# Attention and pair convolution on one core: the outputs of 28 of 32 query chunks turned by a transposing DMA, and VectorE's work put on other steps

## The reference

```python
# layer 0: self-attention over the 4096 positions
f = einsum('kc,bcn->bkn', Wq, xf) + bq        # 32 rows
g = einsum('kc,bcn->bkn', Wk, xf) + bk        # 32 rows
h = einsum('oc,bcn->bon', Wv, xf) + bv        # 256 rows
beta = softmax(einsum('bki,bkj->bij', f, g), axis=1)
x = x + gamma * einsum('bci,bij->bcj', h, beta)
# layer 1: 32 mid channels, all 528 products of two of them, 256 outputs
y = bn_relu(w1 @ gn(x) + b1)
x = x + bn_relu(w2 @ (y[rows] * y[cols]) + b2)
```

## Time and profile before

| | before |
|---|---|
| median of 3 runs | 2097.68 us (2096.98 to 2099.1) |
| the profiled execution, its own time | 2099.17 us |
| its span, first to last instruction | 2097.4 us |
| TensorE busy | 2052.2 us, 98% |
| DVE, ACT, POOL busy | 75%, 78%, 70% |

### The profile page before, as it was taken

One profiled execution on the slowest core, in us unless ns is written; L12 is line 12 of the kernel. 1 busy time (PEld: TensorE's weight loads), 2 busy tenths in 40 slices (PEclk: granted clock), 3 DMA queues, 4 the chain that ended last, 5 costly groups with the idle time before them and its releaser, 6 DMA issues.

```text
span 2097.4 us, 48084 instructions
## 1 busy us (share of the span) xinstructions
PE 2052.2 (98%) x17334; PEld 1612.2 (77%) x17334; DVE 1571.7 (75%) x3491; ACT 1626.0 (78%) x2582; POOL 1464.8 (70%) x2110
## 2 busy tenths in 40 slices
PE   4899999999999999999999999999999999999999
PEld 3688888888877777777877777777787777877854
DVE  8787877778776776877768777776877767676667
ACT  5677877778787878888778788877787777878767
POOL 3265666657677777877768687777867767677766
PEclk9999999999999999999999999999999999999999
DMA  5165777776477797778468687787837776675632
GB/s 191 37 102 96 138 143 144 139 127 118 83 133 126 146 166 150 148 149 162 90 138 144 120 162 141 155 170 138 158 78 135 146 126 138 124 137 92 140 73 80
DMA packets 728269, 271.89 MB, mean 130 GB/s; under 512 B 674240, under 2 KB 681152, under 8 KB 728000
## 3 DMA queue, kind: packets, MB, share of 16 engines
q1 hardware_dynamic: 728032, 268.82, 66.2%
HBM read 77.07 MB, written 19.92 MB: 46 GB/s over the span
## 4 chain that ended last, share of the span: by engine, by line
PE 92%; DVE 3%; ACT 2%; issue 1%; POOL 1%; DMA 1%; SPq 0%; DVEq 0%; ACTq 0%
PE acc L1784 21%; PE acc L1772 20%; PE acc L1773 20%; PE tps L1577 5%; PE acc L1577 5%; PE sps L1597 4%; PE tps L1648 4%; PE acc L1571 3%; PE tps L1650 2%; PE acc L1648 1%; PE tps L1612 1%; PE tps L1558 1%; PE tps L1634 1%; PE acc L1650 1%; PE sps L1547 1%
## 5 line engine op out<-in xcount | busy, mean ns | idle before, releaser
L1162 POOL TENSOR_TENSOR kb<-ks,kb 128x512 f16<-128x512 f32 x630 | 750.6, 1196 | 346.6 <-ACT ks L1345 181.8
L1772 PE MATMUL acc<-hth,kt 128*128 128x257 f16 x2520 | 587.2, 273 | 0.0
L1773 PE MATMUL acc<-htl,kt 128*128 128x256 f16 x2520 | 586.6, 273 | 0.0
L1345 ACT ACTIVATE ks<-ks,kbias,esc 128x512 f32<-128x512 f32 x630 | 506.6, 805 | 0.0
L1333 ACT ACTIVATE ph<-sps,esc 128x512 f16<-128x512 f32 x394 | 269.6, 684 | 276.2 <-PE sps L1597 263.1
L863 DVE TENSOR_SCALAR_CACHE_REDUCE ks<-acc 128x512 f32<-128x512 f32 x378 | 259.6, 687 | 180.7 <-PE acc L1577 178.2
L1784 PE MATMUL acc<-hth,kt 128*128 128x257 f16 x2520 | 385.8, 274 | 0.0
L1772 PE MATMUL acc<-hth,ph 128*128 128x257 f16 x1576 | 367.4, 274 | 0.5 <-ACT ph L1333 0.5
L1773 PE MATMUL acc<-htl,ph 128*128 128x256 f16 x1576 | 366.9, 273 | 0.0
L1784 PEld LDWEIGHTS acc<-hth,kt 128*128 128x128 f16 x2520 | 247.8, 98 | 100.6
L1343 ACT ACTIVATE kb<-ks,kbias,esc 128x512 f16<-128x512 f32 x378 | 305.5, 808 | 21.9 <-DMA kt<-kb 18.3
(11 more groups left out here) (254 smaller groups left out, 3360.4 us busy)
## 6 DMA issues: line engine op xcount, KB each, us to landing
rt<-turned SPq DMA_DIRECT2D x96, 256.0 KB, 4.9
xt<-x SPq DMA_DIRECT2D x46, 512.0 KB, 4.4
xb<-x SPq DMA_DIRECT2D x32, 512.0 KB, 4.9
out<-zt SPq DMA_DIRECT2D x45, 256.0 KB, 2.7
kt<-kb SPq DMA_TRANSPOSE x630, 3.2
yb<-turned SPq DMA_DIRECT2D x36, 128.0 KB, 2.6
rt<-turned SPq DMA_DIRECT2D x72, 64.0 KB, 2.2
turned<-yb SPq DMA_DIRECT2D x12, 256.0 KB, 2.4
```

What stands on the lines that cost most here:

```text
L1162: tt(kb[:, m % KB_RING, 1], ks[:, m % KS_RING], kb[:, m % KB_RING, 0], ALU.subtract).then_inc(kl_ok, 1)
L1345: A(ks[:, m % KS_RING], ks[:, m % KS_RING], ACT.Exp, bias=kbias[:, tile % 2:tile % 2 + 1], scale=esc[:]).then_inc(kp_ok, 1)
L1772: mm(bank[:, 0:C + 1], high[:, q], hth[:, c * QT + q], start=(s8 == 0 and q == 0), stop=False)
L1773: mm(bank[:, 0:C], high[:, q], htl[:, c * QT + q], start=False, stop=False)
```

## The change

In every chunk but the last of an image (28 of 32) the output is no longer turned by TensorE. `divide` writes the fp16 high half of the scaled result into `oth` (the memory of `ot`), a new DVE instruction `output_low` writes the low half in step 5 of the next tile, and SP turns each tile by a transposing DMA into the new buffer `od` (`turn_output`, steps 21, 23 and 31, and step 7 of the next chunk). DVE then adds the high and the low half of each half of the channels to x with four instructions (`finish_turned`, steps 14, 16, 17 and 19) and takes the statistics in steps 21 and 22 (`own_stats`). `od` takes the room of one chunk of x: XR is 13 and no longer 14. The layer-1 low products move from steps 3, 4, 7, 10, 12 to 3, 5, 8, 9, 11, the statistics of the other images to steps 0, 8, 24 and some more, and the early values of the next image to steps 11, 15, 19, 26 of the last chunk with another order of chunks.

```diff
-XR = 14
+XR = 13
+        od = sb("od", [P, QT, 2 * H2, P], f16)
+        oth = ot[:].rearrange("p t c -> p (t c)").bitcast(f16).rearrange("p (t e c) -> p t e c", t=QT, e=2)
-        VORD = (4, 0, 5, 1, 6, 2, 3, 7)
+        VORD = (4, 0, 5, 3, 6, 1, 2, 7)
-        NEXT_STATS = tuple((J, t) for J, ts in ((0, (8, 11, 15)), (1, (11, 15, 21)), (2, (11, 18))) for t in ts)
-        LATER_STATS = ((2, 27), (3, 2), (3, 9), (3, 18), (3, 25), (4, 2), (4, 9), (4, 18), (4, 25), (5, 2), (5, 9), (5, 18),
-                       (6, 22), (6, 29), (7, 4), (7, 11))
+        NEXT_STATS = tuple((J, t) for J, ts in ((0, (8, 16, 24)), (1, (0, 8, 24)), (2, (0, 8))) for t in ts)
+        LATER_STATS = ((2, 24), (3, 0), (3, 8), (3, 24), (4, 0), (4, 8), (4, 24), (5, 0),
+                       (5, 8), (5, 24), (6, 0), (6, 8), (6, 24), (6, 30), (7, 4), (7, 9))
-        V_EARLY = (12, 15, 18, 21)
+        V_EARLY = (11, 15, 19, 26)
 # SP
+            def turn_output(tile):
+                G, k = divmod(tile, QT)
+                sp.wait_ge(ot_low, tiles_lowered(tile))
+                if transfers_before(G):
+                    sp.wait_ge(own_ok, 2 * H2 * transfers_before(G))
+                sp.dma_start_transpose(od[:, k], oth[:, k].rearrange("p e c -> p (e c)")).then_inc(od_in, 16)
...
+                        if J and t == 7:
+                            turn_output(QT * G - 1)
+                        if by_transfer(G) and t in (21, 23, 31):
+                            turn_output(QT * G + (21, 23, 31).index(t))
 # DVE
+            def output_low(tile):
+                k = tile % QT
+                dve.wait_ge(ot_act, tile + 1)
+                V.scalar_tensor_tensor(oth[:, k, 1], acc[tile % 2][:, 0:C], rinv[:, k:k + 1], oth[:, k, 0],
+                                       ALU.mult, ALU.subtract).then_inc(ot_low, 1)
+            def finish_turned(G, e, h):
...
+                own = xb[:, x_slot(b, J), h].rearrange("p (t q) -> p t q", t=QT)
+                V.scalar_tensor_tensor(own, od[:, :, H2 * e + h], vout[:, h:h + 1], own,
+                                       ALU.mult, ALU.add).then_inc(own_ok, 1)
...
-                        if b and n >= 1 and t in (3, 4, 7, 10, 12):
-                            product_low(n - 1, (3, 4, 7, 10, 12).index(t))
-                        if J and t in (5, 8):
-                            finish(G - 1, (t - 5) // 3, 1)
-                        if J and t in (6, 11):
-                            second_stats(G - 1, (t - 6) // 5, 1)
+                        if b and n >= 1 and t in (3, 5, 8, 9, 11):
+                            product_low(n - 1, (3, 5, 8, 9, 11).index(t))
+                        if J and t in (14, 16, 17, 19):
+                            finish_turned(G - 1, *((0, 0), (0, 1), (1, 0), (1, 1))[(14, 16, 17, 19).index(t)])
+                        if J and t in (21, 22):
+                            own_stats(G - 1, t - 21)
 # ACT, divide
+                if transfers_before(G):
+                    act.wait_ge(od_in, 16 * QT * transfers_before(G))
+                if by_transfer(G):
+                    A(oth[:, k, 0], acc[tile % 2][:, 0:C], ACT.Copy, scale=rinv[:, k:k + 1]).then_inc(ot_act, 1)
 # PE
-                            transposed(G - 1, (t - 4) // 3, 1)
...
+                            if by_transfer((tile - 2) // QT):
+                                pe.wait_ge(ot_low, tiles_lowered(tile - 2))
```

More of the change, by code:

```diff
@@ L203, in build @@
         rinv_ok = sem("rinv_ok")
-        ot_act = sem("ot_act")
+        ot_act, ot_low, od_in, own_ok = sem("ot_act"), sem("ot_low"), sem("od_in"), sem("own_ok")
         y_mm, y_ok = sem("y_mm"), sem("y_ok")
@@ L444, in product_at, with by_transfer, transfers_before, tiles_lowered @@
             return rt0[0:rows, grp] if n < SHARED else turn_bank(n, grp)[0:rows, :]
+        def by_transfer(G):
+            return G % NCH != NCH - 1
+        def transfers_before(G):
+            return G - G // NCH
+        def tiles_lowered(tile):
+            return QT * transfers_before(tile // QT) + (tile % QT + 1 if by_transfer(tile // QT) else 0)
         @block.sync
@@ L551, in _ @@
                     n = (b - 1) * NCH + J
+                    G = b * NCH + J
                     nxt = b < LASTB and 3 <= J <= 6
@@ L902, in invert, with own_stats @@
                 V.reciprocal(rinv[:, tile % QT:tile % QT + 1], acc[tile % 2][:, C:C + 1]).then_inc(rinv_ok, 1)
+            def output_low(tile):
[4 more added lines that the diff above has]
+            def finish_turned(G, e, h):
+                b, J = divmod(G, NCH)
+                if e == h == 0:
+                    dve.wait_ge(od_in, 16 * QT * (transfers_before(G) + 1))
+                    dve.wait_ge(bv_ok, G + 1)
+                if e:
+                    dve.wait_ge(own_ok, 2 * H2 * transfers_before(G) + h + 1)
+                own = xb[:, x_slot(b, J), h].rearrange("p (t q) -> p t q", t=QT)
+                V.scalar_tensor_tensor(own, od[:, :, H2 * e + h], vout[:, h:h + 1], own,
+                                       ALU.mult, ALU.add).then_inc(own_ok, 1)
+            def own_stats(G, h):
+                b, J = divmod(G, NCH)
+                dve.wait_ge(own_ok, 2 * H2 * transfers_before(G) + H2 + h + 1)
+                V.bn_stats(bst[:, h, J], xb[:, x_slot(b, J), h])
             def finish(G, h, par):
@@ L1017, in attend @@
                             invert(tile - 1)
+                        if s8 == 5 and tile and by_transfer((tile - 1) // QT) and (J or t >= NCH):
+                            output_low(tile - 1)
                         if s8 == 6 and tile + 2 < TILES:
@@ L1051, in attend @@
                             normed(("qk", b + 1, 2 * (J - 2)))
-                        if b < LASTB and J == NCH - 1 and t in (13, 16, 19, 22):
-                            normed(("v", b + 1, VORD[(13, 16, 19, 22).index(t)]))
+                        if b < LASTB and J == NCH - 1 and t - 1 in V_EARLY:
+                            normed(("v", b + 1, VORD[V_EARLY.index(t - 1)]))
             project()
@@ L1225, in _ @@
                             low(("qk", b + 1, 2 * (J - 3) + 1))
-                        if t in (14, 17, 20, 23) and b < LASTB and J == NCH - 1:
-                            low(("v", b + 1, VORD[(14, 17, 20, 23).index(t)]))
+                        if t - 2 in V_EARLY and b < LASTB and J == NCH - 1:
+                            low(("v", b + 1, VORD[V_EARLY.index(t - 2)]))
                         if t == 20 and b and 1 <= n < SHARED - 1:
@@ L1349, in divide @@
                 act.wait_ge(rinv_ok, tile + 1)
-                k = tile % QT
+                k, G = tile % QT, tile // QT
+                if transfers_before(G):
+                    act.wait_ge(od_in, 16 * QT * transfers_before(G))
+                if by_transfer(G):
+                    A(oth[:, k, 0], acc[tile % 2][:, 0:C], ACT.Copy, scale=rinv[:, k:k + 1]).then_inc(ot_act, 1)
+                    return
                 A(ot[:, k], acc[tile % 2][:, 0:C], ACT.Copy, scale=rinv[:, k:k + 1]).then_inc(ot_act, 1)
@@ L1456, in attend @@
                             high(("qk", b + 1, 2 * (J - 2)))
-                        if b < LASTB and J == NCH - 1 and t in (12, 15, 18, 21):
-                            high(("v", b + 1, VORD[(12, 15, 18, 21).index(t)]))
+                        if b < LASTB and J == NCH - 1 and t in V_EARLY:
+                            high(("v", b + 1, VORD[V_EARLY.index(t)]))
             act.wait_ge(set_dve, mark["scaled_qkv"])
```

12 lines of the change are left out of this document (6 added, 6 removed).

## The result

The changed kernel took 2118.5 us (median of 4 runs, 2116.0 to 2121.3), the kernel before 2098.4 (4 runs, 2097.0 to 2100.1) beside it: ratio 1.0096, 95% interval 1.0078 to 1.0113. It is slower by 20 us, where 12 us less were forecast.

What follows compares the result with a forecast made beforehand. TensorE, busy for 98% of the span, was taken as the bound. -24.1 + 3 + 5.4 + 1.8 + 1.8 = -12.1 us on the profiled 2097.4 gave 2085.3, stated as 2086 from the median; range 2076 to 2096.

Steps and rivals of the forecast that it cites:

- 3, 5.4, 1.8 and 1.8: Forecast losses in us: DVE's additions, early `xt` load, SP at image 0's chunk 6 to 7, chunk 1 of images 1 to 3.
- SP's new transfers: 1.24 us per issue; 1.8 us lost at image 0's chunk 6 to 7, 0.6 each at chunk 1 of images 1 to 3.
- What TensorE loses: Two groups of four transposes in each of 28 chunks, 0.43 us a group: 24.1 us, the whole gain.
- a microsecond taken from TensorE is a microsecond of the kernel: Premise for the attention: TensorE is almost never idle, so time removed there shortens the kernel in full.
- VectorE's work: Additions at 0.96 us and `output_low` at 0.45 add 116 us, taking DVE from 75% to about 81% busy.
- What it costs the end: DVE's added work, tightest in image 0's chunk 3, costs the kernel 3 us, bounds 0 and 9.
- one margin of 2.0 us: Time an unloaded DVE has between finishing a piece and TensorE writing that bank again, from 396.92 to 398.96.
- The second rival: DVE becomes the bound, additions averaging 1.6 us, deciding mean about 1.4: kernel slower, 2105 us; chance 0.08.
- The early load: Image 0, chunk 5: later `xt` load stops ACT, so TensorE waits 5.4 us (4.5 to 6.8) for `ph`.
- The third rival: SP's queue or landing holds `kt` back 0.43 us in most chunks, 12 us more: 2098, no change; chance 0.12.
- The edits costed at nothing: Waits for `output_low` and `od_in`, and the order of value chunks, taken to cost 0 us.

Runs made afterwards that it cites:

- experiment 8: experiment 3 without `output_low` and without the two low additions, so the attention's output is missing: 2082.0 us, ratio 0.9927.
- experiment 3: experiment 1 without its 112 output transfers and the waits for them, the additions reading a zeroed buffer: 2091.8 us, ratio 0.9972.
- experiment 1: The changed kernel with the last statistics of image 0's chunk 5 at step 18 instead of 24: 2112.4 us, ratio 1.0066.
- experiment 2: The kernel before plus 112 transposing transfers at the change's steps into a buffer nobody reads: 2101.7 us, ratio 1.0015.
- experiment 11: The kernel before with the x ring at 13 slots instead of 14 and the matching order of value chunks: 2117.3 us, ratio 1.0093.
- 5: experiment 1 with output transfers merged by two tiles, 56 issues instead of 112, same bytes: 2097.7 us, ratio 0.9999.
- experiment 6: experiment 1 with two additions of a turned chunk instead of four, low halves left out, all transfers kept: 2099.6 us, ratio 1.0010.
- experiment 12: experiment 1 with merged output transfers (half the issues) and the two low-half additions left out: 2087.6 us, ratio 0.9951.
- experiment 4: The kernel before with one TensorE transpose instead of four in each of 56 groups: 2085.9 us, ratio 0.9945.
- 9: The kernel of 5 with statistics moved in chunks 5 and 6, and the turned chunk's statistics in chunk 7: 2096.3 us, ratio 0.9990.
- experiment 7: The change made for only 13 chunks, the rest at the steps of the kernel before, x ring at 13: 2111.2 us, ratio 1.0062.

## Why the prediction was wrong

By runs, the change's way from 2098.4 to 2118.5 us is: 24.1 less on TensorE; 7.7 more with neither transfers nor low halves (experiment 8); 9.8 for the low halves on VectorE (3 against 8); 20.6 for the transfers (1 against 3); 6.1 for the late load (the change against 1). -24.1 + 7.7 + 9.8 + 20.6 + 6.1 = 20.1. The shares hold for this order of removal alone. Taken first, the transfers cost 3.3 us (experiment 2) and the shorter ring 19 (experiment 11); between half the issues and two additions the order matters by only 2.7 us (experiments 1, 5, 6 and 12).

The forecast was of 12 us less. The terms that it added were 3, 5.4, 1.8 and 1.8, and nothing for the rest; the runs show 9.8, 6.1, 20.6 and 7.7. The step that failed most is the price of SP's new transfers, 3.6 us against 20.6, and with it the way of adding up: each term was read against the margins of the kernel before, as if the others left them whole. For the transfers alone 3.6 was near the 3.3 of experiment 2, which lost 1.6 us in chunk 7 of image 0 (1.8 forecast) and 0.7 and 0.3 in chunk 1 of images 1 and 3 (0.6 each).

- **What TensorE loses**: right, 0.87 us a chunk. The premise with it, that "a microsecond taken from TensorE is a microsecond of the kernel", was wrong. Experiment 4 does nothing else and gives 12.4 of 18.1. An engine that is busy for 1493.93 of 1497.00 us says that no one was later than it, not by how much. Chunk 1 of images 1 to 3 did not follow; in image 1 the chain still goes through the `rt` transfer, before and in experiment 4.
- **VectorE's work**: sized well. Its groups in the changed kernel:

```profile
L947 DVE SCALAR_TENSOR_TENSOR xb<-od,vout,xb 128x512 f32<-128x512 f16 x112 | 116.3, 1038 | 0.3
L935 DVE SCALAR_TENSOR_TENSOR ot<-acc,rinv,ot 128x256 f16<-128x256 f32 x112 | 53.5, 478 | 0.0
```

  1.04 us where I took 0.96, 0.48 for 0.45. **What it costs the end** was too small: 3 us with a bound of 9, against 9.8 for the low halves alone. I counted one margin of 2.0 us, at chunk 3 of image 0, which lost nothing. The loss was in its chunks 1, 2, 5 and 7 (experiment 8), which also hold weights, moments or loaded statistics; that these take the margin is argued, not tested. The second rival did not come: its mean of 1.4 was not reached.
- **The early load**: right place, and a price of 5.4 against 6.1 in the kernel's time. That this is so near is partly luck: the stall costs 10.4 us in its own chunk, and 4.0 come back only because the next load moves too (experiment 1). I moved the load behind the spreads and forgot the two output transfers, which push the spreads too (402.02, not 397.67); I followed `ph`, while TensorE stood for `gst`, which ScalarE makes behind it; and I priced no loss of clock.
- **SP's new transfers**: the step that failed most, 3.6 us against 20.6. The price of an issue was right (1.24); I charged it at four places and not in steps 21 to 31 of chunks 3 to 6, where SyncE also issues twelve spreads and, in images 1 and 2, layer-1 transfers. The third rival's mechanism (0.12) is what came, but in a few chunks: by experiments 1 and 3, 2.0 to 4.6 us each in chunks 5 and 7 of images 1 and 2, and 3.7 in chunk 6 of image 0, not 0.43 in all.
- **The edits costed at nothing**: the ring of 13 and the order of the chunks. I looked only at the ring's effect on one load. Experiment 11 shows 19 us if nothing is moved. How the 7.7 us divide between the ring, the moves and the failed premise no run isolates. SyncE in experiment 6 is still 2.7 us later than in experiment 2 at the table's place; 2.5 of them are two plain issues that held it for 1.70 and 1.81 us, where 0.43 and 0.59 are usual. What made them long is open.

## What to carry to other kernels

When the bound engine is given less to do, its margins shrink with it: before counting the saving, read for each queue that gets new work the slack at its most crowded place (landing against use), not its mean share. Here the queue paid per issue and hardly per byte: merge transfers before moving them. And count the memory that a change takes: a ring one slot shorter can cost as much as the change was to give.

## What the chip showed beyond that

**The granted clock can halve when TensorE has stood still.** Stands of 8.59 us (changed kernel), 6.31 (experiment 11), 2.57 (9) and 2.14 (1) came with a granted clock of 0.50, the lower of the two levels, 1.2 GHz, for 10.2, 6.8, 3.4 and 3.4 us (from 405.0 and 998.5 in the two long ones, within the stand, and at its end or 1.1 us behind it in the short ones). All five stands of 5.9 us and more did so. Of the shorter ones the length alone does not decide: one of 2.03 us in experiment 7 was followed by 0.50, while this one, another of 2.27 and one of 2.27 in experiment 12 were followed by a clock of 1.00 (experiment 6, a row and its window):

```profile
409.28 0.39 PE L1636 MATMUL tps<-fst,gst 96*128 96x512 f16 x1 [2.26 <-DVE mx L876]
407.00:416.00 9.00, 6.74 (x59) 5.40 (x59) 7.40 (x20) 6.60 (x11) 4.51 (x4) 1.00 1.15 208
```

At 0.50 the products take 0.42 us for 0.27. Working at half clock from 410.43 to 415.2, TensorE does 2.4 us of work in 4.8, so by this estimate the first stand costs 11.0 us, not 8.6. The Trainium skill (page "TensorE: Matmul & The Clock Gate", section "Part 1: The HAM clock gate") says that the throttled state is the default and activity releases it; by that rule a long stand is paid twice, and the rows of the long stands agree.

**A transposing transfer holds SyncE nearly the same for 1 or 2 tiles**: 1.234 and 1.299 us at the median, and a `kt` transfer, as large as two tiles, for 1.237. The merged ones land later, 3.4 us after the issue and not 3.0.

**VectorE and GpSimd slow each other.** GpSimd's busy time rose from 1464.8 to 1521.4 us with no instruction added, while additions that read SBUF twice took 725 to 1645 ns. The transfers are not the reason: with them alone it is 1470.9 us (experiment 2), with VectorE's work alone 1526.4 (experiment 3), and with half the additions and no low halves 1505.0 (experiment 8). The shorter ring alone leaves it at 1466.7 (experiment 11).
